# Six expert tiles of a fused attention and mixture-of-experts kernel, run between the last attention step and the last routing

## The reference, cut to what matters

```python
h = jnp.concatenate([image_filter(x), txt_weight[x_txt]], axis=1)          # 16 x 333 x 256
h = h + windowed_attention(layernorm(h), Wq, bq, Wk, bk, Wv, bv, Wo, bo, pos_bias)
x = layernorm(h).reshape(-1, 256)                                          # 5328 tokens
scores = softmax(x @ gate_w.T)
top_scores, sel = top_k(scores, 2)
# tokens sorted by expert; y = (silu(x @ w1[e]) * (x @ w3[e])) @ w2[e], inner width 512
out = h + scatter_add(token, y * score)
```

## Time and profile before

| | |
|---|---|
| median of three runs | 1263.39 us |
| the profiled execution | 1263.12 us |
| its span, first to last instruction | 1261.2 us |
| PE busy | 1149.9 us (91%) |
| DVE busy | 837.0 us (66%) |
| ACT busy | 706.7 us (56%) |
| POOL busy | 594.6 us (47%) |
| mean granted clock of TensorE | 0.973 |

### The profile page before, as it was taken

One profiled execution on the slowest core, in us unless ns is written; L12 is line 12 of the kernel. 1 busy time (PEld: TensorE's weight loads), 2 busy tenths in 40 slices (PEclk: granted clock), 3 DMA queues, 4 the chain that ended last, 5 costly groups with the idle time before them and its releaser, 6 DMA issues. The chain is left out here.

```text
span 1261.2 us, 34362 instructions
## 1 busy us (share of the span) xinstructions
PE 1149.9 (91%) x10510; PEld 946.9 (75%) x10511; DVE 837.0 (66%) x4259; ACT 706.7 (56%) x1977; POOL 594.6 (47%) x751
## 2 busy tenths in 40 slices
PE   2499999999999999999998449999999999999996
PEld 1367666766666766766666349999999999999995
DVE  3478989988998899998888444444444444444442
ACT  1399999999999999999999211111111111111110
POOL 7555656666567656765454323322332332232232
PEclk9799999999999999999999669999999999999998
DMA  5654445654354434533341533232323323323232
GB/s 135 172 159 138 139 136 167 172 149 129 116 150 138 115 100 140 160 107 87 113 135 35 162 110 47 48 50 46 49 47 49 47 46 50 46 46 50 46 50 30
DMA packets 98394, 123.31 MB, mean 98 GB/s; under 512 B 15544, under 2 KB 87416, under 8 KB 95192
## 3 DMA queue, kind: packets, MB, share of 16 engines
q1 hardware_dynamic: 75880, 89.96, 25.4%
q0 software_dynamic: 18576, 24.47, 11.5%
q10 hardware_dynamic: 3808, 7.34, 1.8%
HBM read 69.35 MB, written 46.07 MB: 92 GB/s over the span
## 5 line engine op out<-in xcount | busy, mean ns | idle before, releaser
L703 ACT ACTIVATE probs<-probs,neg_max 128x128 f32<-128x128 f32 x1280 | 402.5, 398 | 1.5 <-DVE neg_max L818 0.7
L818 DVE CUSTOM_DVE_ANT_0 probs<-s_bank,nbias 128x128 f32<-128x128 f32 x1280 | 293.7, 285 | 56.7 <-PE s_bank L1105 51.7
L741 ACT ACTIVATE v_all<-s_bank 128x512 f32<-128x512 f32 x91 | 54.4, 598 | 286.1 <-PE s_bank L1261 259.3
L1116 PE MATMUL t_bank<-ident,probs 128*128 128x128 f32 x1280 | 194.0, 274 | 0.2 <-ACT probs L703 0.2
L1276 PE MATMUL o_bank<-stacks,v_all 128*128 x728 | 172.4, 380 | 0.3 <-issue 0.2
L652 POOL DMA_INDIRECT out_dram<-wq_sb,nbias x46 | 75.9, 1651 | 194.3 <-DVE wq_sb L1026 172.7
L652 POOL DMA_INDIRECT out_dram<-wk_sb,nbias x45 | 73.3, 1629 | 175.0 <-DVE wk_sb L1026 172.1
L696 ACT ACTIVATE probsT<-t_bank 128x512 f32<-128x512 f32 x240 | 142.3, 593 | 20.7 <-PE t_bank L1116 18.5
L1032 DVE TENSOR_TENSOR v_all<-v_all,t_bank 128x512 f32<-128x512 f32 x91 | 62.6, 688 | 129.7 <-PE t_bank L1261 129.7
L1132 PE MATMUL o_bank<-probsT,v_all 128*32 128x128 f32 x2560 | 136.3, 285 | 7.3 <-ACT probsT L696 4.0
L1276 PEld LDWEIGHTS o_bank<-stacks,v_all 128*128 128x128 f32 x728 | 131.3, 190 | 15.4 <-issue 1.2
(11 more groups left out here) (160 smaller groups left out, 1988.7 us busy)
## 6 DMA issues: line engine op xcount, KB each, us to landing
stacks<-qk_parts SPq DMA_DIRECT2D x192, 166.5 KB
qk_parts<-parts_flat SPq DMA_DIRECT2D x192, 83.2 KB
nbias<-expert_slots SPq DMA_DIRECT2D x91, 129.0 KB
w_sb<-in_L_ffn_w_dram ACTq DMA_DIRECT2D x14, 512.0 KB
v_all<-v_all SPq DMA_DIRECT2D x64, 96.0 KB
x_here<-in_x_dram SPq DMA_DIRECT2D x16, 256.0 KB
out_dram<-h_res SPq DMA_DIRECT2D x16, 256.0 KB
stacks<-in_L_ffn_w_dram SPq DMA_DIRECT2D x8, 512.0 KB
```

Source lines behind the costliest of these rows:

```text
L703: ins = act.activation(seg, seg, ACT.Exp, bias=neg_max[:, r, i:i + 1], scale=-1.0)
L741: act.activation(hidT[r % 2], s_bank[:, r % 2, :], ACT.Silu).then_inc(silu_ready, 1)
L818: ins = dve.tensor_tensor_reduce(probs[:, r, i * WIN:(i + 1) * WIN], s_bank[:, k % 2, i * WIN:(i + 1) * WIN], nbias[:, h, :], 1.0, BIG, AL ...
L1116: mm = pe.transpose(t_bank[:, (k - 3) % 2, i * WIN:(i + 1) * WIN], probs[:, r, i * WIN:(i + 1) * WIN], ident[:, :])
```

## The change

The table is split in two. `EARLY = 6` tiles come from a first table, made of the routing of the first 14 batches (`EARLY_BATCHES`). For each expert only tiles that are already full are taken (the count of rows is rounded down), in the order of the experts, until there are six. The second table has the other 85 tiles, the remaining ones of those experts first shifted by the tiles used. There are still 91 tiles.

- DVE computes the first table in step 15, in pieces at k = 5, 7, 9, 11, 13 and 15, 24 linked operations, and at k = 19 copies the weights of tile 0. The running sum over experts becomes three shifted additions instead of seven single ones.
- SP in step 15 loads w3 of expert 7, five of the w2, stores the batch's rows, and loads w1 of expert 7. In step 16, as soon as the last scores are read, it loads the rows of tiles 0 to 3, then the other three w2, stores batch 15 and loads the rows of tiles 4 and 5, each after tile 0 or tile 1 has been added.
- PE, ACT, DVE and POOL get the work of tiles 0 to 4, and the first half of tile 5's, written by hand into steps 16 and 17 (below). The second table is computed at step 17, k = 3, in two pieces, with products of tile 4 and tile 3 between them.
- The scatter (0,1) moves from k = 5 to k = 8 in step 16. The two buffers of `ctxT` and the two of `up_w` swap places.

```diff
+EARLY = 6
+EARLY_BATCHES = B - 2
+MAIN = MT - EARLY
 # SP
+                if b == B - 1:
+                    sp.wait_ge(res_ready, B)
+                    sp.wait_ge(xn_ready, B * 3)
+                    sp.dma_start(w3_sb[:, E - 1], ...).then_inc(expert_weights_in, 16)
+                    sp.wait_ge(scores_done, (B - 1) * G)
+                    for e in range(5):
+                        load_down(e)
                     store_h2()
+                    sp.wait_ge(wo_done, (B - 1) * 2)
+                    sp.dma_start(w1_sb[:, E - 1], ...).then_inc(expert_weights_in, 16)
+                if b == B:
+                    sp.wait_ge(max_ready, B * G)
+                    sp.wait_ge(early_ready, 1)
+                    sp.wait_ge(scattered, 96 * EARLY_BATCHES)
+                    for t in range(RING):
+                        load_tile(t, t)
+                    for e in range(5, E):
+                        load_down(e)
+                    sp.wait_ge(h2_stored, 32 * (B - 1))
+                    store_h2()
+                    for t in range(RING, EARLY):
+                        load_tile(t, t % RING)
 # POOL
-                    if tail2 and k == 5:
+                    if tail2 and k == (8 if b == B else 5):
                         scatter(0, 1)
+                    if b == B + 1 and k == 9:
+                        add_tile(2, 2)
+                    if b == B and k == 14:
+                        pool.wait_ge(h2_stored, 32 * (B - 1))
+                        add_tile(0, 0)
+                    if b == B and k == 17:
+                        add_tile(1, 1)
 # ACT
+                    if b == B and k == 4:
+                        gxT_tile(0, 0)
+                        gxT_tile(1, 1)
+                    if b == B and k == 6:
+                        silu_tile(0, 0)
+                    if b == B and k == 11:
+                        silu_tile(1, 1)
+                        gxT_tile(2, 0)
+                        gxT_tile(3, 1)
+                        silu_tile(2, 2)
+                    if b == B + 1 and k == 3:
+                        silu_tile(3, 3)
+                        gxT_tile(4, 0)
+                        gxT_tile(5, 1)
+                        silu_tile(4, 0)
 # DVE
+                    if b == B - 1:
+                        early_table(k)
+                    if b == B and k == 5:
+                        dve.wait_ge(pT_done, B * G)
+                        up_weights(1, 1)
+                    if b == B and k == 6:
+                        hid_tile(0, 0)
+                    if b == B and k == 13:
+                        dve.wait_ge(qk_done, 4 * B)
+                        up_weights(2, 0)
+                        hid_tile(1, 1)
+                        y_tile(0, 0)
+                        up_weights(3, 1)
+                    if b == B and k == 16:
+                        hid_tile(2, 2)
+                        up_weights(4, 0)
+                        y_tile(1, 1)
+                    if b == B - 1 and k == 19:
...
+                        up_weights(0, 0)
+                    if b == B + 1 and k == 3:
+                        dve.wait_ge(prefix_read, B * 2)
+                        dve.tensor_copy(region_end_i[:, :], region_end[:, :]).then_inc(pads_ready, 1)
+                        hid_tile(3, 3)
+                        y_tile(2, 2)
+                        up_weights(5, 1)
+                        main_table_start()
+                        hid_tile(4, 0)
+                        y_tile(3, 3)
+                        main_table_end()
+                        up_weights(6, 0)
 # PE
+                        if b == B:                      # k == 8, before the output projection
+                            pe.wait_ge(gxT_ready, 2)
+                        if b == B:                      # k == 17, before the transposition for the gate
+                            pe.wait_ge(gxT_ready, 4)
+                    if b == B and k == 18:              # behind the gate
+                        up_half(3, 1, 0)
+                    if b == B and k == 4:
+                        pe.wait_ge(early_ready, 1)
+                        gx_tile(0, 0)
...
+                        gx_tile(1, 1)
+                    if b == B and k == 6:
+                        pe.wait_ge(max_ready, B * G)
+                        up_tile(0, 0)
+                    if b == B and k == 11:
+                        up_tile(1, 1)
+                        pe.wait_ge(down_weights_in, 16 * E)
+                        down_tile(0, 0)
+                        pe.wait_ge(h2_ready, B * NT)
+                        gx_tile(2, 2)
+                        gx_tile(3, 3)
+                        up_tile(2, 0)
+                    if b == B and k == 17:
+                        down_tile(1, 1)
+                    if b == B + 1 and k == 2:
+                        up_half(3, 1, 1)
+                        down_tile(2, 2)
+                        pe.wait_ge(prefix_read, B * 2)
+                        gx_tile(4, 0)
+                        gx_tile(5, 1)
+                        up_tile(4, 0)
+                        down_tile(3, 3)
+                        up_tile(5, 1)
+                        down_tile(4, 0)
-            gx_tile(0, 0)
-            up_tile(0, 0)
-            gx_tile(1, 1)
-            run_tiles(pe, tile_step)
+            pe.wait_ge(table_ready, 1)
+            gx_tile(6, 2)
+            run_tiles(pe, tile_step, EARLY - 1)
```

More of the change, by code:

```diff
@@ L50 @@
 MT = TOKENS * K // P + E
+EARLY = 6
+EARLY_BATCHES = B - 2
+MAIN = MT - EARLY
+PAD = E // 2
 RING = 4
@@ L297, in run_steps, with run_tiles @@
                 step(b, b % 2)
-        def run_tiles(eng, step):
-            for t in range(2 * RING):
+        def run_tiles(eng, step, first):
+            for t in range(first, 2 * RING):
                 step(t, t % RING)
@@ L511, in fill_pads, with add_tile @@
                 pool.dma_start(out[TOKENS:TOKENS + P, :], pad_rows[:, 0:D]).then_inc(pads_in, 16)
+            def add_tile(t, r):
+                pool.wait_ge(y_ready, t + 1)
+                if later(t, 1):
+                    wait_apart(pool, y_added, t * 16)
+                pool.indirect_dma_start(out[:, :],
+                                        bass.IndirectOffsetOnAxis(g_rows[r][:, D + 1:D + 2].bitcast(I32), 0),
+                                        y_sb[r], None, compute_op=ALU.add).then_inc(y_added, 16)
             def step(b, par):
@@ L646, in _ @@
             pool.wait_ge(h2_stored, 32 * B)
[L648 to L656, removed]
+            run_tiles(pool, add_tile, 3)
             pool.wait_ge(y_added, 16 * MT)
@@ L774, in normalise, with link @@
                                       ALU.subtract, ALU.mult).then_inc(done, 1)
+            steps = [0]
+            def link(ins):
+                steps[0] += 1
+                ins.then_inc(table_step, 1)
+                dve.wait_ge(table_step, steps[0])
+            tiles_to = running[:, 1, PAD:PAD + E]
+            def whole_tiles(extra):
+                link(dve.scalar_tensor_tensor(out=n_rows[:, :], in0=region_end[:, :], scalar=float(extra),
+                                              in1=tile_base[:, :], op0=ALU.add, op1=ALU.subtract))
+                link(dve.tensor_copy(n_rows_i[:, :], n_rows[:, :]))
+                link(dve.tensor_scalar(n_rows_i[:, :], n_rows_i[:, :], P.bit_length() - 1, None,
+                                       ALU.logical_shift_right))
+                link(dve.tensor_copy(n_tiles[:, :], n_rows_i[:, :]))
@@ new lines, in running_sum, with expert_of @@
+            def running_sum():
+                for i, s in enumerate((1, 2, 4)):
+                    src, dst = running[:, i % 2, :], running[:, 1 - i % 2, :]
+                    link(dve.tensor_tensor(dst[:, PAD:PAD + E], src[:, PAD:PAD + E], src[:, PAD - s:PAD + E - s], ALU.add))
+            def expert_of(n):
+                ge, number = tab_ge[:, 0:n, :], tile_no[:, 0:n]
+                link(dve.tensor_tensor(ge, number.unsqueeze(2).to_broadcast([P, n, E]),
+                                       tiles_to.unsqueeze(1).to_broadcast([P, n, E]), ALU.is_ge))
+                link(dve.tensor_reduce(tab_e[:, 0:n], ge, AX.X, ALU.add))
@@ L776, in step, with tile_step @@
+            def tile_step(t, r):
+                hid_tile(t, r)
+                y_tile(t - 1, (r - 1) % RING)
+                if not isinstance(t, int) or t + 2 < MT:
+                    up_weights(t + 2, r % 2)
             def step(b, par):
```

280 lines of the change are left out of this document (149 added, 131 removed).

## The result

The changed kernel takes 1236.49 us (median of four runs, 1234.75 to 1238.22) against 1264.12 us of the kernel before in the same comparison: ratio 0.9778, 95% interval 0.9766 to 0.979, so 27.6 us (26.5 to 29.6 by the interval) less. Predicted were 1238.0 us and a range of 1231.5 to 1246.0. The profiled execution took 1235.95 us; its span is 1233.8 us, against 1261.2.

The account below looks back on a forecast made before the run. Tiles were bound by PE's own work (5.52 us each), the gap before them by small chained steps. Tile 6 begins at 751.3 instead of 776.82, 25.5 us sooner: 1263.12 becomes 1237.6, plus 0.27 gives 1238.0 us; range 1231.5 to 1246.

Parts of the forecast that it names:

- Step 15: Last attention step: the first table's 24 DVE operations cost 1.7 us (bounds 0.5 and 4), tile 0's weight copy 0.4.
- Tile 0 and the projection: From the last transposition of heads through tile 0 to the output projection's end: 712.8, 2.4 us later than before.
- 1.5 us extra, as if 3 us ran at 1.2 GHz: Allowance for a lowered PE clock at tile 0, whose products take 3.57 us at full clock, 7.1 at 1.2 GHz.
- From there to the gate: Projection's end to gate's end: 9.9 us of PE's queue plus 3.9; gate ends at 726.6, 4.6 us later than before.
- From the gate to tile 6: Three chains behind the gate: slots, PE and second table, the table latest; tile 6 could start at 748.7.
- G: The time at which the gate ends, forecast as 726.6; later marks are counted from it.
- The start at 1.2 GHz: Tile 6 starts at 1.2 GHz behind PE's wait: 2.6 us lost, bounds 0 and 3.6, so counted as begun at 751.3.
- The rule on the shared port: DVE's fp32 copies lock GpSimd out throughout: tile 5's copy would count 1.3 us, not 0.4; sum 1238.5.
- B: Rival, more hidden: no clock fall before tile 0, cheaper step 15, tile 6 loses less; 1231 to 1234, chance 0.12.
- A: The case as summed: 1234 to 1242 us, chance 0.62.
- D: Rival: clock stays at 1.2 GHz through both steps, inserted pieces double, no change, 1263 us; chance 0.02.
- C: Rival: queues cost more, step 15 in full, tile 0 slow, hand-overs 3 to 6 us; 1242 to 1252, chance 0.19.
- E: Rival, slower: the 85 tiles lose their rhythm; at 0.6 us more a tile the time is 1288; chance 0.04.

Follow-up runs that it names:

- e4: Kernel before with 24 linked operations nobody needs on DVE in the last attention step, no early tiles: 1264.38 us, ratio to before 1.0007.
- e8: Kernel before with 48 linked operations nobody needs on DVE in the last attention step, no early tiles: 1269.12 us, ratio to before 1.0034.
- e1: Changed kernel with the whole second table computed before tile 4's product and tile 3's scaling: 1232.53 us, ratio to before 0.9755.
- e7: Changed kernel with ten more linked operations of 0.205 us each inside the second table: 1236.51 us, ratio to before 0.9774.
- e9: Changed kernel with only tile 3's scaling moved behind the second table, tile 4's product before its second piece: 1232.93 us, ratio to before 0.9755.
- e12: Repeat of e7, the changed kernel with ten more linked operations in the second table: 1237.16 us, ratio to before 0.9782.
- e5: Changed kernel with 15 unread products on PE behind the down products of tile 4: 1233.40 us, ratio to before 0.9744.
- e6: Kernel before with unread PE products as long as each inserted piece, at its place, no early tiles: 1262.90 us, ratio to before 0.9984.
- e11: The changed kernel run again, unaltered: 1236.17 us, ratio to before 0.9781.
- e2: Changed kernel with 30 unread products on PE behind the down products of tile 4: 1236.49 us, ratio to before 0.9779.

## Why the prediction was right, and where it was off

- **The frame held.** A tile is worth PE's 5.52 us, and the gain is read off at the start of tile 6. Predicted there: 25.5 us; measured at tile 7: 28.1. That the time came out within 1.5 us of 1238.0 is in part luck: 0.7 us of the gain went in the tile stage, and the kernel before measured 1264.12 in this comparison, where the sum started from 1263.39. (The sum gives 1237.9; 1238.0 is its rounding.)
- **Step 15** was priced too high: 1.7 us for the links where 0.4 were measured in e4 and in the changed kernel; the bound below, 0.5, was nearer. The guess that ACT, a group behind, hides little was wrong for one table and right for two (e8). The copy for tile 0 was 0.4 predicted; from the logits of batch 14 to the last transposition of heads there are 8.29 us instead of 7.73, so 0.6.
- **Tile 0 and the projection.** The term "1.5 us extra, as if 3 us ran at 1.2 GHz" was nothing: the clock did not fall before the tiles. The projection ended at 710.43, not at 712.8. The prediction also read the clock of the kernel before too simply, as low from 702.5 to 747.0. It had been back at 1.00 in between:

```profile
709.50:712.50 3.00, 0.92 (x5) 0.34 (x3) 2.65 (x9) 0.00 (x0) 1.03 (x2) 1.00 0.41 139
```
- **From there to the gate,** 9.9 + 3.9 us predicted; 710.43 to 723.69 is 13.3. PE's queue was the later one, as argued: the normalised rows were ready at 718.95, and PE took them at 720.26. The gate ended 1.7 us later than before, not 4.6: 2.4 us for the two reasons above, 0.5 here.
- **From the gate to tile 6** the sum was right nearly to the tenth: table ready at G + 18.1 (measured 18.1), rows used and tile 6 begun at G + 22.1 (22.2), and the slots just ahead of the table (G + 17.3 predicted; they came at L + 17.0 in the changed kernel, 1.1 us before the table, and at 16.5 in e1). One step of the slots' sum is missing in the prediction: 4.5 + 8.71 + 2.3 is 15.5 and not 16.4; the rest is the second between the region ends and the first empty block (725.93 and 727.12 in the kernel before). That the second table is the last chain is shown by SP's waits and by e1, and by the traces of e7, e9 and e12.
- **The start at 1.2 GHz** cost 6.37 - 3.57 = 2.8 us (2.6 predicted), shown by e5 to be the clock.
- **The rule on the shared port** changed nothing. Tile 5's weight copy lay beside a scatter of 1.08 us, where its neighbours took 0.98 to 0.99, so it cost 0.1 us, not the 0.4 taken from the additions. The Trainium skill (SBUF — State Buffer, "Who interferes with whom") has the lock last for the whole instruction, and the weight copy is two instructions of 0.69 us each, so the 1.3 us that the prediction took by that rule was too much in any case; the scatter's 0.1 us is far below a block of 0.69 as well, but GpSimd's small arithmetic agrees with the rule (last section). Since the slots were not the last chain, the time could not show it.
- **Rivals.** Of B's three parts, two came true (clock before tile 0, step 15) and one did not, and that third is the 2.8 us of tile 6. The time, 1236.5, lies inside A's 1234 to 1242. D (1.2 GHz throughout) fell: the clock was 1.00 from 700 to 740, because the inserted work itself kept it there. C's hand-overs did not appear, nor did E's lost rhythm: 474.0 us from tile 8 to the end against 473.3.
- **The signs.** The table was what SP waited for, and no tile was at 1.2 GHz before tile 6, as forecast; the gate ended 1.7 us later instead of 4 to 5. One sign of being wrong did show, "a tile above 5.6 us after tile 10": it was ill chosen, as the kernel before has four such tiles.

By e1 the change still left 3 to 4 us: one line moved gives 1232.5 and 1233.5 us. The table in the middle (e9, 1232.9) and e5's unread products, which cover the wait (1233.4), reach the same within what these runs can tell.

## What to carry to other kernels

Where one stage is bound by an engine's own work and a gap ahead of it is bound by a chain of small hand-overs, whole units of that work belong into the gap, even in front of steps on the critical chain: at full clock those steps themselves become shorter and pay for most of what they wait. Afterwards look for the last wait that remains ahead of the dense stage; it costs its length and the clock behind it, so order the queues such that what ends it comes first. And put extra small operations only where the engine still waits: here the first 5 us were nearly free, and with the next 5 the step grew by 4.2.

## What the runs showed of the hardware that was not expected

- A wait of TensorE between dense work of 0.9 and of 1.15 us left the granted clock at 1.00 (e5, e1). Behind one of 1.38 us (e6) and one of 2.17 us (e9) it fell during the next tile, was at 0.50 for 3.4 us, and the tile took 5.5 instead of 3.84 us. Behind 3.5 us it was at 1.2 GHz when the tile began (changed kernel, 6.37 us). Behind a wait 2.1 us longer still, the tile took less, 5.4 and 5.5 us (e7, e12): the clock was low for 6.8 us in all of these, and the longer wait had used up more of them.
- GpSimd's small arithmetic waited for VectorE's weight copies. Root steps that take 0.20 us took 0.59 and 0.52 us where a copy was already running (a third, at 716.78, took 0.51), and so they did in e1 and e11:

```profile
713.02 0.19 POOL L512 TENSOR_TENSOR root_tmp<-rstd 128x3 f32<-128x3 f32 x1
713.14 1.29 DVE L914 COPY parts_flat<-w_sb 128x1024 f32 x2 [0.86 <-issue]
713.29 0.59 POOL L514 TENSOR_TENSOR root_tmp<-root_tmp,var_eps 128x3 f32<-128x3 f32 x1
...
713.97 0.52 POOL L516 TENSOR_SCALAR root_tmp<-root_tmp 128x3 f32<-128x3 f32 x1
```

```profile
L914 DVE COPY parts_flat<-w_sb x2: 686/690/693, 713.1 to 713.7; 128x1024 f32 x2
```

  The two copies took 0.69 us each and ended at 713.83 and 714.43; the two steps ended at 713.88 and 714.49, 0.05 and 0.06 us behind a copy. This fits a lock that lasts for one copy instruction, not for the pair. It cost the root 1.0 us in all, but no time: the normalised rows were ready at 718.95, and PE took them only at 720.26.

- The last attention step's length varied by up to 0.9 us for the same instructions (37.93 us in e1, 38.79 in e2), and the longer ones are those with 3.4 us at 1.2 GHz in it. The stages before it varied by 2 us, which is why marks within a trace tell more here than spans.
